# Two attentions in one kernel: value matmuls grouped by two steps, and the unit loop written out

## What is computed

```
attn = softmax(q @ k.T * scale)          # per batch and head: 1024 x 1024
(block 1 only: attn = attn * triu(ones)) # applied after the softmax
out  = attn @ v                          # 1024 x 8 per head
```

## Time and profile before

| what | value |
|---|---|
| median of 3 runs | 2227.5 us (2225.45 to 2233.21) |
| span of the profiled execution | 2223.8 us |
| first attention: first to last value group | 144.1 to 517.4 us |
| second attention: first to last value group | 1321.9 to 1710.9 us |

### The profile page before, as it was taken

The page is one execution under the profiler, slowest core; times in us unless marked ns, Lnnn a source line. Parts: engine busy times, 40 slices in busy tenths (PEclk is TensorE's granted clock), DMA queues, the critical chain, the costliest instruction groups (busy, mean ns, idle before and its releaser), DMA issues. The chain is left out here.

```text
span 2223.8 us, 34232 instructions
## 1 busy us (share of the span) xinstructions
PE 1952.8 (88%) x11540; PEld 1135.8 (51%) x11568; DVE 1485.3 (67%) x2689; ACT 1172.0 (53%) x2385; POOL 570.8 (26%) x491
## 2 busy tenths in 40 slices
PE   6389999996899987999988389999997689999997
PEld 4023323323777755887755123333332467777776
DVE  4688888852656544666544388887881578787787
ACT  3137766774555552555543317666666245545554
POOL 2530000000333320433310221111222035354444
PEclk9569999998899997999999659999999689899999
DMA  1200000001000000000000210000001100000000
GB/s 59 93 30 23 22 26 26 17 1 56 15 6 6 6 0 15 6 6 6 6 0 0 83 44 25 25 25 26 25 4 15 54 1 0 0 0 0 0 0 19
DMA packets 48000, 42.91 MB, mean 19 GB/s; under 512 B 36093, under 2 KB 39549, under 8 KB 44941
## 3 DMA queue, kind: packets, MB, share of 16 engines
q1 hardware_dynamic: 47256, 39.32, 5.3%
q10 hardware_dynamic: 576, 2.16, 0.3%
q0 software_dynamic: 64, 0.07, 0.0%
HBM read 32.79 MB, written 8.39 MB: 19 GB/s over the span
## 5 line engine op out<-in xcount | busy, mean ns | idle before, releaser
L823 DVE TENSOR_REDUCE att_neg_max<-psum 128x1 f32<-128x1024 f32 x512 | 603.4, 1219 | 161.0 <-PE psum L701 156.4
L805 ACT ACTIVATE att_probs<-psum 128x512 f32<-128x512 f32 x1024 | 532.9, 604 | 337.7 <-PE psum L724 337.6
L701 PE MATMUL psum<-att_k_op,att_q_op 72*128 72x512 bf16 x1024 | 339.2, 416 | 61.4 <-PEq L357 51.1
L724 PE MATMUL psum<-att_q_op,att_k_op 74*128 74x512 bf16 x1024 | 325.5, 389 | 19.2 <-ACT att_probs L805 8.2
L1734 ACT ACTIVATE moe_hidden<-psum,moe_b 128x512 f32<-128x512 f32 x256 | 168.8, 689 | 137.3 <-PE psum L74 116.9
L724 PEld LDWEIGHTS psum<-att_q_op,att_k_op 74*128 74x128 bf16 x1024 | 81.9, 97 | 289.2 <-ACT att_probs L805 224.9
L741 PE MATMUL psum<-att_probs,att_v 128*32 128x512 f32 (+2 forms) x1664 | 205.2, 563 | 0.5 <-ACT att_sums L796 0.4
L701 PEld LDWEIGHTS psum<-att_k_op,att_q_op 72*128 72x128 bf16 x1024 | 97.0, 101 | 190.7 <-DVE att_neg_max L823 69.9
L62 DVE CAST moe_hidden_high<-moe_hidden 128x512 fp32r<-128x512 f32 x256 | 148.8, 598 | 42.2 <-ACT moe_hidden L1734 42.2
L911 POOL TENSOR_TENSOR att_diag<-att_probs,att_triangle 128x512 f32<-128x512 f32 x64 | 82.4, 1287 | 320.1 <-ACT att_probs L805 298.6
L1289 ACT ACTIVATE win_p<-win_sm,win_nb,win_q_scale 128x192 f32<-128x192 f32 x256 | 137.6, 539 | 42.6 <-DVE win_nb L1350 41.6
(11 more groups left out here) (226 smaller groups left out, 3176.9 us busy)
## 6 DMA issues: line engine op xcount, KB each, us to landing
att_q_op<-qk_parts SPq DMA_DIRECT2D x48, 192.0 KB
att_k_op<-qk_parts SPq DMA_DIRECT2D x48, 192.0 KB
win_w_pair<-in_win_wj SPq DMA_DIRECT2D x9, 320.0 KB, 2.7
win_table<-in_xpos SPq DMA_DIRECT2D x1, 2048.0 KB, 10.0
moe_w<-in_moe_w SPq DMA_DIRECT2D x2, 1024.0 KB, 5.8
x_ch<-in_x ACTq DMA_DIRECT2D x1, 1024.0 KB, 5.4
qk_parts<-rot_hi SPq DMA_DIRECT2D x4, 256.0 KB, 2.5
qk_parts<-rot_mid SPq DMA_DIRECT2D x4, 256.0 KB, 2.7
```

Source lines behind the costliest of these rows:

```text
L701: last = pe.matmul(buf[:, half * CHUNK:(half + 1) * CHUNK], q_op[r][0:SPLIT_ROWS, j, t * P:(t + 1) * P], k_op[r][0:SPLIT_ROWS, j, half * C ...
L724: mm = pe.matmul(st_bank[(r + e) % 3], k_op[r][:, j, t * P:(t + 1) * P], q_op[r][:, j, half * CHUNK:(half + 1) * CHUNK], start=True, stop= ...
L805: ins = act.activation(probs[:, s % PB, j, :], st_bank[(r + e) % 3], ACT.Exp, scale=scale)
L823: ins = dve.tensor_reduce(neg[:, t, j:j + 1], buf, AX.X, ALU.max, negate=True)
```

## The change

On TensorE the values of two steps are issued together: in each even step the values of the two steps before it, in odd steps none. In step 0 of a unit these are the last two steps of the unit before; after the last unit the last two steps follow its scores. On all four engines the loop over units 1 to 6 is replaced by plain repetition, so that all 8 units are written out one after another and every wait compares with a constant.

```diff
         def loop(engine, body):
-            body(0, None, 0, 0)
-            with engine.Fori(0, (UNITS - 2) // RING) as i:
-                for u in range(RING):
-                    body(i * RING + (u + 1), i * RING + u, i + (u + 1) // RING, (u + 1) % RING)
-            body(UNITS - 1, UNITS - 2, (UNITS - 1) // RING, (UNITS - 1) % RING)
+            for it in range(UNITS):
+                body(it, it - 1 if it else None, it // RING, it % RING)
...
-                    if s >= 1:
+                    if s % 2 == 0 and s:
+                        values(it, r, s - 2)
                         values(it, r, s - 1)
-                    elif before is not None:
+                    elif s == 0 and before is not None:
+                        values(before, (r - 1) % RING, STEPS - 2)
                         values(before, (r - 1) % RING, STEPS - 1)
...
                 if is_last(it):
+                    values(it, r, STEPS - 2)
                     values(it, r, STEPS - 1)
                     entry(3, base, "turn", 1, it)
```

## The result

The changed kernel takes 2252.2 us (median of 4 runs, 2243.53 to 2256.53), the kernel before 2226.47 in the runs made beside it: a ratio of 1.0114, interval 1.0084 to 1.0143. It is slower by 1.1%. 2246 had been forecast, with 2228 to 2268 around it. The profiled execution has a device time of 2249.68 us and a span of 2247.2, 23.4 above the span before.

A forecast was written before the change was run, and what follows sets the result against it. TensorE in its written order was taken to bound a step, VectorE close behind (2.35 of 2.83 us). Loop's turn -11.6, paired loop units +20.4 and edges +10 sum to +18.8 us: 2227.5 to 2246, range 2228 to 2268.

The forecast's parts named there:

- The loop's turn: Where the old loop jumps back, TensorE idles and drops its clock; removing this saves 5.2 and 6.4 us, together -11.6.
- The register waits: Loop waits comparing with registers cost up to 0.07 us a step in 192 steps; contained in the rebuilt step, not added.
- The ring stall: VectorE's two buffers stall TensorE 0.46 us per two steps: 5.93 us, or 6.81 with a "turn"; +20.4 in loop units.
- the first rival: VectorE releases faster, ScalarE binds next, about 2203 us; change even at a reduction interval of 1.09 us; chance 0.14.
- Pairs with a "rows" entry: Two-step pairs in loop units containing a "rows" entry, priced like ordinary pairs at +0.11 us each.
- The second value group: In the paired value block the second group needs 0.88 us on TensorE instead of 1.00, making 1.88 for two.
- The edges: First and last units: unit 0 loses near 2 us, the last unit 3, so +5 per attention, +10 together.
- ScalarE's wait: In the last unit ScalarE starves during the longer value block: pairs take 5.22 us against 4.80, seven by 0.42.
- the clock rival: TensorE's clock falls to the lower level in the paired last unit of both attentions: +29 us, 2275; chance 0.05.
- The sum: Whole kernel: -11.6 + 20.4 + 10 = +18.8 us, taking the time from 2227.5 to 2246 us.
- The ring does not stall PE: VectorE releases faster in paired steps; ScalarE binds, pairs take 5.64 us, 6.13 with a "turn"; 2203 us; chance 0.14.
- Net nothing: The stall exists, but a second value group or restart cheaper by 0.15 a pair offsets it: 2229 us; chance 0.10.

The follow-up runs named there:

- the single-step kernel: Against the kernel before: all units written out as straight code, values still issued one step at a time; 2202.07 us, ratio 0.9894.
- the cut reductions: Maxima inside units over 512 of 1024 columns, exponential's scale a thousandth: on the changed kernel 2215.35 us, on written-out units with single steps 2207.61 us.
- the second measurement: Against the kernel before: units 1 to 6 as body of a one-pass loop, which came out nearly as the written-out single-step code; 2207.51 us.

## Why the prediction was right, point by point

**The loop's turn, -11.6 us.** Right. No unit of the changed kernel is longer than its neighbours (49.19 each), and the pairing in the loop is 12.3 us slower than the changed kernel (2264.5 against 2252.2); the two turns in that run cost 5.4 and 7.0 us.

**The register waits.** They had no term of their own: the pair was built from durations without them and set against 2.91 a step. That holds. In single steps they are worth 46.74 against 47.77 and 48.61 against 49.65 per unit, 12.4 us over the twelve units. With pairing they are worth nothing.

**The ring stall, pair of 5.93 and 6.81.** Right in kind, and measured at 5.88 and 6.75. The term mis-sized is the interval between reductions. I took 1.18 from the stretch ahead of the units, which runs at a granted clock of 0.50. Inside the units it is (4.62 - 1.22) / 3 = 1.13, which the earlier trace rows already showed: 2.35 for two. With 1.13 the fourth entry comes 3.04 after the first; 3.05 was measured. The 1.28 from a reduction's start to the entry behind it held (209.65 to 210.93), so the wait fell with the interval once, not twice as the first rival's break-even at 1.09 has it. Pairs with a "rows" entry, priced like ordinary ones at +0.11, cost +0.14 (6.09 against 2.91 + 3.04). So twelve loop units lost 6 x (49.19 - 47.77) + 6 x (51.08 - 49.65) = 17.1 us, not 20.4.

**The second value group, 0.88.** Right: the block to the next score is 1.85 (206.72 to 208.57) where 1.88 was summed.

**The edges, +10.** Too small. From the first score to the last "turn" the first attention grew from 383.2 to 398.6 us and the second from 399.7 to 411.2, together by 26.8; less 17.1, plus 11.6, that leaves 21.3 for units 0 and 7. Unit 7, from the last "max" entry to the last "turn", takes 52.6 us against 43.6 in the first attention and 51.8 against 46.2 in the second: 14.6 us, where 6 had been forecast. The other 6.7 belong to unit 0, where 4 had been forecast; at its start the lower clock lasts by several us longer in some profiles than in others, so this part is not cleanly measured. In unit 7 ScalarE's wait is as forecast (pairs of 5.22). What was missing is the clock rival, to which I had given 0.05 and kept out of the sum. It happened in part: four pairs of unit 7 in the first attention and two in the second ran wholly or partly at 1.2 GHz, 1.4 to 1.9 us longer each than such pairs at the full clock, and one more was 0.2 longer, 9.8 us in all. Undoing the pairing there gave 12 us in the medians and 14.3 in the profiled unit 7; doing it alone cost 13.0 in the profiled unit 7, and 16.7 or 11.2 in the medians, by which measurement of the single-step kernel it is set against. Whether differing numbers of such pairs also explain why the four runs lie as far apart as 2243.5 and 2256.5 was not traced; the mean granted clock is highest in the fastest of them (0.912, against 0.905 to 0.908).

**The sum.** -11.6 + 17.1 + 21.3 = 26.8 us in the two attentions; outside them the profiled span is 3.4 us shorter than in the profile before, where nothing was changed. The forecast had 18.8 for the attentions, 8.0 too little: the ring was priced 3.3 too high and the edges 11.3 too low. That the time still came out only 6 us above 2246 is in part luck. The two errors go against each other, and the 3.4 us outside were not foreseen; the other way, the median lies 5.0 us above the profiled span, where 3.7 had been added.

**The rivals.** "The ring does not stall PE" is refuted by the cut reductions, which give 37 us in the paired kernel and none in the single one. "Net nothing" needed 0.15 a pair from a cheaper second group or restart; 0.03 of it was there (1.85 for 1.88).

## What to carry to other kernels

Grouping one engine's work saves a switch (0.2 us here) but turns a steady supply for the other engines into bursts; count how many buffers the neighbours have against the longer block before grouping, because a mean load of 2.35 of 2.83 says nothing of a ring with two places. Measure the halves of a compound edit apart: here writing out gave -1.1% and pairing on top of it +2.3% (2252.2 over 2202.1; 2.0% over the second measurement, 2207.5), and the version with the first alone is the one to keep. Take a duration from the stretch where it will apply, not from the cleanest one.

## What the runs showed of the hardware

The granted clock of TensorE fell inside work that was never idle for long: in unit 7, paired, where the matmul rows name waits of at most 0.26 us, it went to a mean of 0.72 in 494 to 518 us and came back to full in the same unit, with the same instructions. With single steps, where a step has PE at work for 1.88 of 2.40 us in place of 3.6 of 5.22, it stayed at 1.00 in unit 7 of all five profiles taken. The Trainium skill (TensorE: Matmul & The Clock Gate, "A second HAM failure mode: psum-queue depth-cycling") tells of a kernel whose matmul groups cycle through PSUM banks with short idle times between them, and whose clock goes down and up for it. These rows look like that; which of the idle times does it was not tested.

A turn of the long loop stalled PE for 2.0 to 3.3 us and cost 5 to 7 us with the lower clock after it, in both kernels that have it. What PE waits for there is not shown: the trace names no releaser. Eight units of straight code showed no such stall.
